# Third attention of a fused transformer block: value rows on TensorE in groups of two at every second step

## The reference, cut to what matters

```
def _L1_attn_ref(x, w_qkv):
    ...
    att = jnp.einsum('bhqd,bhkd->bhqk', q, k) * scale
    causal = jnp.tril(jnp.ones((T, T), dtype=bool))
    att = jnp.where(causal, att, -jnp.inf)
    att = jax.nn.softmax(att, axis=-1)
    out = jnp.einsum('bhqk,bhkd->bhqd', att, v)
```

## Time and profile before

| | |
|---|---|
| median of 3 runs | 1818.73 us (1810.61 to 1827.36) |
| the profiled execution, its own time | 1816.31 us |
| its span, first to last instruction | 1814.6 us |
| busy TensorE / VectorE / ScalarE / GpSimd | 1598.9 / 1293.7 / 1128.7 / 674.7 us |
| the third attention's loop over items | about 1344 to 1715 us of the span |

### The profile page before, as it was taken

How to read it: one execution, slowest core, us unless ns; L and a number is a source line. 1 busy time by engine, 2 the same in 40 slices (tenths; PEclk the granted TensorE clock), 3 DMA queues, 4 the chain that set the end, 5 groups by cost and what they waited for, 6 DMA issues and landing times. The chain is left out here.

```text
span 1814.6 us, 36604 instructions
## 1 busy us (share of the span) xinstructions
PE 1598.9 (88%) x12310; PEld 696.2 (38%) x12310; DVE 1293.7 (71%) x2458; ACT 1128.7 (62%) x1788; POOL 674.7 (37%) x1223
## 2 busy tenths in 40 slices
PE   5888888597899999999999888897589999999787
PEld 3422222243344444444444554454333333333233
DVE  6688888676667777777772346664499999999064
ACT  6699999443046565555556434322628888888655
POOL 6566766676313232323222001102513333333373
PEclk9799999799979999999999999988899999999998
DMA  8643434257323131413210400000712222222201
GB/s 236 157 69 58 69 68 135 55 134 174 59 36 78 44 83 43 78 48 72 54 43 25 170 28 1 0 0 1 227 31 52 52 52 52 52 52 70 61 14 47
DMA packets 92080, 125.99 MB, mean 69 GB/s; under 512 B 24533, under 2 KB 64085, under 8 KB 91686
## 3 DMA queue, kind: packets, MB, share of 16 engines
q1 hardware_dynamic: 89814, 121.30, 28.9%
q10 hardware_dynamic: 2096, 2.47, 0.4%
HBM read 76.03 MB, written 47.58 MB: 68 GB/s over the span
## 5 line engine op out<-in xcount | busy, mean ns | idle before, releaser
L1174 DVE TENSOR_REDUCE o_sb<-ps 128x1 f32<-128x512 f32 (+3 forms) x864 | 706.7, 863 | 150.5 <-PE ps L968 143.5
L1065 ACT ACTIVATE q_buf<-ps 128x1024 f32<-128x1024 f32 (+1 forms) x768 | 567.8, 833 | 232.0 <-PE ps L937 230.8
L1127 POOL TENSOR_SCALAR_AFFINE_SELECT q_buf<-q_buf 128x256 f32<-128x256 f32 x432 | 212.9, 515 | 380.9 <-ACT q_buf L1065 320.4
L1065 ACT ACTIVATE pr_buf<-ps 128x1024 f32<-128x1024 f32 (+1 forms) x384 | 286.1, 834 | 63.1 <-PE ps L937 63.0
L989 PE MATMUL ps<-q_buf,v_buf 128*9 128x512 f32 (+7 forms) x2880 | 306.1, 515 | 13.5 <-POOL q_buf L1127 11.7
L937 PE MATMUL ps<-q_buf 48*128 48x512 bf16 (+7 forms) x1536 | 269.6, 330 | 21.6 <-ACT q_buf L1065 5.4
L937 PE MATMUL ps<-q_buf,k_buf 49*128 49x512 f32 (+3 forms) x1536 | 280.4, 492 | 0.0
L1127 POOL TENSOR_SCALAR_AFFINE_SELECT pr_buf<-pr_buf 128x256 f32<-128x256 f32 x336 | 166.3, 520 | 268.6 <-ACT pr_buf L1065 227.3
L937 PEld LDWEIGHTS ps<-q_buf 48*128 48x128 bf16 (+1 forms) x1536 | 78.7, 94 | 255.9 <-ACT q_buf L1065 133.4
L989 PE MATMUL ps<-pr_buf,v_buf 128*9 128x512 f32 (+7 forms) x1728 | 158.3, 459 | 17.5 <-POOL pr_buf L1127 17.5
L937 PEld LDWEIGHTS ps<-q_buf,k_buf 49*128 49x128 f32 x1536 | 143.3, 188 | 71.2 <-issue 46.8
(11 more groups left out here) (184 smaller groups left out, 1750.3 us busy)
## 6 DMA issues: line engine op xcount, KB each, us to landing
q_buf<-qm_d SPq DMA_DIRECT2D x32, 384.0 KB, 6.7
qm_d<-pr_buf SPq DMA_DIRECT2D x80, 128.0 KB, 2.4
o_d<-pr_buf SPq DMA_DIRECT2D x16, 512.0 KB, 2.7
q_buf<-o_d SPq DMA_DIRECT2D x8, 1024.0 KB, 5.0
q_d<-q_buf SPq DMA_DIRECT2D x48, 128.0 KB, 2.1
k_d<-q_buf SPq DMA_DIRECT2D x48, 128.0 KB, 1.9
k_buf<-km_d SPq DMA_DIRECT2D x32, 192.0 KB, 6.8
q_buf<-q_d SPq DMA_DIRECT2D x60, 96.0 KB
```

The source lines that it names most:

```text
L1065: nc.scalar.activation(units(i, g, WIDE * e, WIDE), ps[:, bank:bank + WIDE, :], ACT.Exp, scale=scale).then_inc(s_e, 1)
L1127: nc.gpsimd.affine_select(out=blk, in_=blk, compare_op=ALU.is_ge, fill=0.0, base=0, pattern=[[0, 2], [1, P]], channel_multiplier=-1)\
L1174: nc.vector.tensor_reduce(to, sc, AX_X, ALU.max).then_inc(s_mr, 1)
```

## The change

For "a1" the fixed rule "row g-2 at the end of step g" is replaced by a table: row 0 at the end of step 2, rows 1 and 2 of step 4, rows 3 and 4 of step 6, rows 5 and 6 of step 8, rows 7 and 8 at the end of step 1 of the next item (written as 10). Steps 0, 3, 5 and 7 have no value row. "a0" and "am" keep the old rule. Nothing is added or taken away, and the order of scores and maxima stays. At the end, `rest` still runs rows 7 and 8 of the last item.

```
+            VALUES_AT = {2: (0,), 4: (1, 2), 6: (3, 4), 8: (5, 6), 10: (7, 8)}
+            def values_at(g):
+                if clip or latent:
+                    return [g - PLAG]
+                return [r for at, rows in VALUES_AT.items() for r in (rows if at == g else
+                                                                      [r - ROWS_P for r in rows] if at == g + ROWS_P else ())]
...
                         for g in range(ROWS_P):
                             ahead = max_row(g, last) if has_max else None
+                            rows = values_at(g)
                             for step, which in ROW_ORDER:
...
-                                elif g >= PLAG:
-                                    value_row(n, i, g - PLAG)
-                                elif last != 0:
-                                    value_row(n - 1, i - 1, g - PLAG + ROWS_P)
+                                else:
+                                    for r in rows:
+                                        if r >= 0:
+                                            value_row(n, i, r)
+                                        elif last != 0:
+                                            value_row(n - 1, i - 1, r + ROWS_P)
```

## The result

The changed kernel takes 1886.66 us (median of 4 runs, 1883.18 to 1891.97) against 1818.51 before: 3.8% slower, ratio 1.0378, interval 1.0344 to 1.0411. In the second set of experiments it was measured again on another occasion, 1887.86 us and 1.0375 (1.0313 to 1.0438). I had forecast 1862, from 1844 to 1884. The direction was right, and the loss is 1.6 times what I had worked out.

A forecast was written before the change was run, and what follows sets the result against it. VectorE was taken as the bound in the third attention. Pauses 37.0, ScalarE 2, steps without maxima 3.6 and clock 1 sum to 43.6 us, giving 1859.9 on the profiled execution; with 2.4 for the median, 1862 us, range 1844 to 1884.

The forecast's parts named there:

- the term for the clock: Third attention, mostly its last item with emptier steps: half clock on TensorE adds 1 us (nothing to 4).
- VectorE is the bound, and a pause is 1.56 + G - 2.3: Third attention: VectorE waits by this rule, G being value-row time between s3 and next scores; sum +37.0 us.
- The length of a group: Value rows on TensorE: two full rows take 1.85 us, rows 3+4 2.28, rows 1+2 1.42; following rows save 0.11.
- ScalarE: Third attention: ScalarE runs dry during a group, and the output copy in step 5 delays an exponential; +2 us.
- The steps without maxima: Last 13 steps, where TensorE and ScalarE pace each other: groups, the copy and the end add 3.6 us.
- The rival of the clock: Third attention: clock falls to half in every item, about 1.4 us once an item, 20 us, so 1882; chance 0.14.

The follow-up runs named there:

- the run with the clock held: The changed kernel with score products s2 and s3 run three times each in the steps without value rows: 1861.36 us, ratio 1.0252.

## Why the prediction was wrong, and where it was right

The step that failed is the term for the clock, +1 in the sum; the runs show about 34 us in its place. The terms one by one:

- *VectorE is the bound, and a pause is 1.56 + G - 2.3.* Right. At full clock the three groups give 1.11, 1.50 and 1.10 us where the rule gave 1.11, 1.54 and 1.11, the group at step 4 gives none, and the sum of waits is 52.5 us against 50.9. That the stretch came out so close has some luck in it: the 0.15 us behind step 2, put at nothing, are 2 us in 14 items, and VectorE's own records cover less in the changed kernel (21.56 us in the item from 1523.02 to 1548.52, 21.73 in the item of the earlier trace rows), which takes 2.4 away again. That TensorE can't use its free steps is seen in the same rows: two double banks are all the lead there is.
- *The length of a group,* 1.85 for two rows: 1.84. So a row behind a row does save 0.11 us, which is too little to matter here.
- *ScalarE,* +2: the stretch at full clock is +36.6 against 37.0 + 2, and the pauses behind steps 5 and 6 are no longer than the rule gives. No run shows this term; it was nothing or nearly so.
- *The steps without maxima,* +3.6: 2.3 against before as it stands, up to 4.0 if the clock that before lost there is taken out.
- *The clock,* +1 (nothing to 4). This is the term that failed. It measured 24.0 us in the stretch with maxima and 9.5 to 11.2 in the one without (the lower figure if 1.7 of it is counted as lost before already), 34 to 35 together. All other terms came to 42.6 and measured 38.9 (36.6 + 2.3), or up to 40.6; with -3.4 elsewhere that makes the 70.6 of the two profiles (38.9 + 35.2 - 3.4 = 70.7).
- *The rival of the clock* had the mechanism and, by chance more than by working, the time: I had priced it at 1.4 us once an item, 20 us, and it was 1.6 us, 13 times, about 21 of the 24.0 us. The 11 us of the last steps it had no price for. I gave it 0.14, with the argument that a stretch of 3.9 us is shorter than the 6 us in item 0. But the rows that I had were two falls after stretches with little for TensorE to stream, one of them in steps that still had a value row each; they bounded nothing from below. The last 13 steps were the plainest case: they lost the clock once before, with a value row in every step, and I took +1 for leaving every second step there without one. With the 20 us of this rival in the sum and some 10 for the last steps the forecast would have been 1892, near the 1886.66 measured.

The Trainium skill, TensorE: Matmul & The Clock Gate, speaks in its section on HAM oscillation of idle gaps between bursts, and in "What's actually happening" of a gate set by how busy the engine has been recently. In the changed kernel's trace no wait of TensorE's products from 1360 to 1739 us is over 0.6 us, and in the steps from 1495.9 to 1505.5 its records cover 8.16 of 9.60 us, and still the clock falls. With more products in the steps without values it stays at 1.00 (the run with the clock held). So here it is the second sentence that holds. How much activity is enough, the runs don't show: one step without values cost the clock at step 5 and not at step 3.

## What to carry to other kernels

When instructions of an in-order engine are bunched, work out for each bunch how far the consumer can be ahead in buffers (here two double banks, 2.3 us); everything beyond shows in full, and the time saved in the empty steps is waited away. Evenness has a second value on TensorE: the empty steps between bunches lowered its clock, so that the bunch itself ran at half speed, just where it was on the path, which was half of the loss.

## What the runs showed of the hardware that I had not expected

- More matrix products made the kernel faster: 256 repeated score units took 26.5 us off, because the granted clock stayed at 1.00 instead of 0.93 in the stage. The reported busy share of TensorE doesn't foretell it: 8.16 of 9.60 us were busy before this fall, and 17.21 of 22.00 in the kernel before while the clock was 1.00 all through the earlier trace rows.
- A fall of the clock nearly doubles the value rows (4.38 us against 2.28 for one group), and it is irregular: in both profiles of the changed kernel 13 of the 42 groups with a pause behind them are hit, at other places in each.
